# Normal rows and second-batch rows on VectorE instead of GpSimd, and two constant matmuls fewer, in an attention and mixture-of-experts kernel

## What is computed

```python
xn = _layernorm(x)
x = x + attention(xn) + ffn(xn)
# attention: 16 heads of 128, biases on q, k, v and o, causal softmax
# ffn(h):    x1 = rmsnorm(h, ln1_w); q, k with rotary embedding, 16 q heads, 4 k and v heads
#            r = h + causal_attention(x1) @ wo
#            y = rmsnorm(r, ln2_w); 4 of 32 experts for each token by softmax(y @ gate_w.T) + bias_e
#            r + sum of the weighted experts + one shared expert
```

## Time and profile before

| | |
|---|---|
| median of three runs | 797.4 us (795.85, 797.7, 797.4) |
| the profiled execution | 794.62 us, its span 792.8 us |
| mean granted TensorE clock | 0.986 |
| busy over the span | PE 750.2, DVE 539.9, ACT 489.9, POOL 494.1 us |
| chain that ended last, by engine | PE 76%, DVE 9%, ACT 6%, POOL 6% |
| normal rows on POOL (L621) | 8 rows, 1210 to 1228 ns each |
| second batch's rows on POOL (L607) | 4 rows, 1203 to 1814 ns each |
| first batch's rows on DVE (L1416) | 4 rows, 483 to 901 ns each |

### The profile page before, as it was taken

The page is one execution under the profiler, slowest core; times in us unless marked ns, Lnnn a source line. Parts: engine busy times, 40 slices in busy tenths (PEclk is TensorE's granted clock), DMA queues, the critical chain, the costliest instruction groups (busy, mean ns, idle before and its releaser), DMA issues.

```text
span 792.8 us, 14431 instructions
## 1 busy us (share of the span) xinstructions
PE 750.2 (95%) x4657; PEld 668.6 (84%) x4657; DVE 539.9 (68%) x1667; ACT 489.9 (62%) x1219; POOL 494.1 (62%) x564
## 2 busy tenths in 40 slices
PE   7759779999999999999998899999999999999997
PEld 4649669889888989888977788999999999999996
DVE  5647567979788797766678876665555565555564
ACT  3646557778777776667443566566556665566652
POOL 6957667867786778434433677366555865656553
PEclk9988999999999999999999999999999999999999
DMA  6000000000010129900100254077786777667634
GB/s 189 8 14 14 21 8 27 14 20 23 14 41 28 40 67 327 280 15 14 41 14 27 76 177 143 30 167 180 177 219 146 190 176 178 145 149 170 143 56 143
DMA packets 103523, 77.51 MB, mean 98 GB/s; under 512 B 6982, under 2 KB 102298, under 8 KB 103450
## 3 DMA queue, kind: packets, MB, share of 16 engines
q1 hardware_dynamic: 92114, 63.13, 27.7%
q0 software_dynamic: 10752, 12.74, 9.6%
q10 hardware_dynamic: 584, 0.73, 0.3%
HBM read 51.75 MB, written 24.82 MB: 97 GB/s over the span
## 4 chain that ended last, share of the span: by engine, by line
PE 76%; DVE 9%; ACT 6%; POOL 6%; issue 2%; DMA 1%; ACTq 0%; DVEq 0%; POOLq 0%
PE j L870 19%; PE ob L870 11%; PE zb L870 10%; PE s L870 10%; PE t L1011 7%; PE j L965 4%; ACT probs L1186 3%; PE j L973 2%; DVE probsT L1461 2%; PE zb L965 2%; PE ob L965 2%; POOL probs L700 1%; PE s L996 1%; POOL acc_a L621 1%; DVE probs L1446 1%
## 5 line engine op out<-in xcount | busy, mean ns | idle before, releaser
L700 POOL TENSOR_SCALAR probs<-probs,inv_sum 128x128 f32<-128x128 f32 x240 | 141.2, 600 | 152.8 <-DVE inv_sum L1452 148.1
L1186 ACT ACTIVATE probs<-probs,neg_max 128x128 f32<-128x128 f32 (+3 forms) x256 | 143.1, 559 | 126.9 <-DVE neg_max L1446 125.3
L1446 DVE CUSTOM_DVE_ANT_0 probs<-s,mask 128x128 f32<-128x128 f32 (+3 forms) x256 | 120.1, 485 | 40.4 <-PE s L996 27.4
L870 PE MATMUL s<-k_heads,q_heads 128*128 128x256 f32 (+2 forms) x576 | 140.6, 366 | 7.4 <-DVE neg_max L1446 7.0
L753 POOL DMA_INDIRECT moe_sum_dram<-late,slot_tokens x64 | 100.7, 1574 | 39.4 <-ACT late L1274 28.3
L1461 DVE TENSOR_TENSOR probsT<-t,probsT 128x384 fp32r<-128x384 f32 (+2 forms) x192 | 101.2, 548 | 11.1 <-ACT probsT L1201 11.0
L870 PEld LDWEIGHTS s<-k_heads,q_heads 128*128 128x128 f32 x576 | 93.2, 194 | 13.8 <-DVE neg_max L1446 10.0
L1201 ACT ACTIVATE probsT<-t 128x384 fp32r<-128x384 f32 (+2 forms) x192 | 90.1, 488 | 18.1 <-PE t L1011 17.8
L1011 PE MATMUL t<-ident,probs 128*128 128x128 f32 x640 | 94.7, 275 | 3.4 <-POOL probs L700 2.8
L1011 PEld LDWEIGHTS t<-ident,probs 128*128 128x128 f32 x640 | 74.8, 141 | 12.5 <-POOL probs L700 4.7
L870 PE MATMUL zb<-probsT,v_heads 128*128 128x512 f32 (+2 forms) x351 | 68.9, 340 | 1.4 <-DVE probsT L1461 0.9
(11 more groups left out here) (256 smaller groups left out, 1600.1 us busy)
## 6 DMA issues: line engine op xcount, KB each, us to landing
x_slots_dram<-mask SPq DMA_DIRECT2D x1, 8480.0 KB, 37.7
late<-x_slots_dram SPq DMA_DIRECT2D x32, 265.0 KB, 4.7
late<-in_L_ffn_weg_dram SPq DMA_DIRECT2D x64, 128.0 KB
late<-in_L_ffn_weu_dram SPq DMA_DIRECT2D x64, 128.0 KB
late<-in_L_ffn_wed_dram SPq DMA_DIRECT2D x64, 128.0 KB
moe_sum_dram<-mask SPq DMA_DIRECT2D x2, 1152.0 KB, 7.0
raw_qk<-in_L_ffn_wq_dram SPq DMA_DIRECT2D x16, 128.0 KB, 2.2
raw_o<-in_L_ffn_wo_dram SPq DMA_DIRECT2D x8, 256.0 KB, 2.7
```

The lines of the kernel that those rows point to most:

```text
L700: pool.tensor_scalar(piece, piece, rinv[:, u % 2, i:i + 1], 1.0, ALU.mult, ALU.mult).then_inc(p_norm, 1)
L870: m = pe.matmul(dst, lhs(a), rhs(b), start=first and i == 0, stop=last_ and i == 2, skip_group_check=skip)
L1186: act.activation(piece, piece, ACT.Exp, bias=nmax[:, u % 2, i:i + 1], scale=-1.0, accum_out=rsum[:, u % 2, i:i + 1]).then_inc(e_done, 1)
L1446: ve.tensor_tensor_reduce(pr[:, u % 2, P_OFF[i]:P_OFF[i] + width], bS[i % 2][:, 0:width], mask_t[:, S - width:S], INV_SCALE, BIG, ALU.add, ...
```

## The change

The rms rows of the second batch and the normal rows are written by VectorE. The two functions leave GpSimd's block and its `step`; on VectorE a function `rms_rows(b)` serves both batches and is called for batch 1 at the end of window -2, and `normal_rows(n)` stands in the rotary branch of `step`, ahead of `z_part(n)`. The semaphores `rows_of_b1` and `normal` are gone: the readers ask VectorE's own counter `ln_step`. The second call of `keep_busy`, with a count of two, is gone. The routing of tokens to experts is not touched.

```diff
@@ the numbers of VectorE's steps
-                    [(what, b) for what in ("var", "eps")] + [("xr", t) for t in tiles if b == 0]):
+                    [(what, b) for what in ("var", "eps")] + [("xr", t) for t in tiles]):
             LN[key] = len(LN) + 1
+    for t in range(NT):
+        LN["xn", t] = len(LN) + 1
@@ GpSimd
-            def second_rows(tiles):
-
-                for t in tiles:
-                    pool.tensor_scalar(xr[1][:, t - TB, :], accB[:, t, :], mv[:, t, 0:1], rstd[:, 1, t:t + 1],
-                                       ALU.subtract, ALU.mult).then_inc(rows_of_b1, 1)
-
...
-            def normal_rows(n):
-
-                if n in XN_UNITS:
-                    p = XN_UNITS.index(n)
-                    for t in (2 * p, 2 * p + 1):
-                        pool.tensor_scalar(accA[:, t, :], accB[:, t, :], mv[:, t, 0:1], rstd[:, 0, t:t + 1],
-                                           ALU.subtract, ALU.mult).then_inc(normal, 1)
...
                         first_powers(1)
                         q_sin(n, it)
-                        second_rows(range(TB, TB + 2))
                         q_lo(n, it)
-                        second_rows(range(TB + 2, NT))
                     weights(job, it)
...
                     normal_power()
-                normal_rows(n)
                 if n in (GS + 1, 2 * GS + 1):
                     pool.wait_ge(bc_in, 32)
-                    pool.wait_ge(normal, NT)
+                    pool.wait_ge(ln_step, LN["xn", NT - 1])
@@ TensorE
             last.then_inc(cx_mm, 1)
-            keep_busy(2)
...
-                        if b == 0:
-                            pe.wait_ge(ln_step, LN["xr", t])
-                        else:
-                            pe.wait_ge(rows_of_b1, t + 1)
+                        pe.wait_ge(ln_step, LN["xr", b * TB + t])
...
                 elif kind == "XN":
-                    pe.wait_ge(normal, 2 * v + 2)
+                    pe.wait_ge(ln_step, LN["xn", 2 * v + 1])
@@ VectorE
+            def rms_rows(b):
+
+                ve.wait_ge(ln_pow, b + 1)
+                for t in tiles_of(b):
+                    did(ve.tensor_scalar(xr[b][:, t - b * TB, :], accB[:, t, :], mv[:, t, 0:1], rstd[:, 1, t:t + 1],
+                                         ALU.subtract, ALU.mult), "xr", t)
+
+            def normal_rows(n):
+
+                if n in XN_UNITS:
+                    p = XN_UNITS.index(n)
+                    ve.wait_ge(ln_pow, B + 1)
+                    for t in (2 * p, 2 * p + 1):
+                        did(ve.tensor_scalar(accA[:, t, :], accB[:, t, :], mv[:, t, 0:1], rstd[:, 0, t:t + 1],
+                                             ALU.subtract, ALU.mult), "xn", t)
+
             variances(0)
-            ve.wait_ge(ln_pow, 1)
-            for t in range(TB):
-                did(ve.tensor_scalar(xr[0][:, t, :], accB[:, t, :], mv[:, t, 0:1], rstd[:, 1, t:t + 1],
-                                     ALU.subtract, ALU.mult), "xr", t)
+            rms_rows(0)
...
                         rope_sum(q, it)
                         k_lo(k, it)
+                        rms_rows(1)
                     if n == -1:
...
                 for ch in k_last:
                     k_lo(ch, it)
+                normal_rows(n)
                 z_part(n, it)
```

More of the change, by code:

```diff
@@ L375, in attention_pair_moe_kernel @@
         bias_added, table_in = sem("bias_added"), sem("table_loaded")
-        rows_of_b1, normal = sem("second_rows"), sem("normal_rows")
         cx_mm, cx_ev = sem("const_turned"), sem("const_kept")
```

## The result

| | before | after |
|---|---|---|
| median of four runs each, us | 796.62 (795.01 to 797.7) | 778.48 (778.03 to 778.96) |
| the profiled execution, us | 794.62 | 778.87 |
| its span, us | 792.8 | 777.1 |
| mean granted TensorE clock | 0.986 | 0.991 |
| busy PE / DVE / POOL, us | 750.2 / 539.9 / 494.1 | 747.7 / 548.3 / 478.8 |

The ratio after to before is 0.9774, interval [0.9753, 0.9795]: faster by 2.3%. The forecast was 777.4 us with a range of 773.5 to 785.0. By medians 18.1 us are gained where 20.0 were forecast; by the two profiled executions it is 15.75. What follows goes by those two executions, since only they have positions. One of the twelve executions of constants_only, in the experiments, took 941.65 us at a granted clock of 0.75 and is not in the ratio given there. L12 is now line 12 of the changed kernel, or of the kernel of the experiment.

The account below looks back on a forecast made before the run. TensorE was taken as bound by waits before 112 us, mostly for GpSimd's normal rows, and by its matmuls after. 12.8 + 5.5 + 1.3 + 0.4 = 20.0 us took the median from 797.4 to 777.4 us, range 773.5 to 785.0.

Parts of the forecast that it names:

- The normal rows: Units 0, 1, 4, 5: on VectorE at 0.65 us a row, TensorE's waits shrink to 0, 0.8, 0, 1.2; gain 12.8 us.
- The clock behind the waits: TensorE's clock stays high after the first, second and fourth turning of the normal rows; gain 5.5 us.
- I expect no fall after waits this short: At the turnings, waits of 0 to 1.2 us leave TensorE's clock high, so 3.45 us become 1.85 three times.
- The second batch's rows: At the start, moving four rows to VectorE brings the first mask forward and spares the last mask a wait; gain 1.3 us.
- 4 x 0.65 = 2.6 us: Four second-batch rows on VectorE before the first mask, which then starts at 23.5 instead of 24.29; gain 0.8 us.
- The second step: The second batch's last mask no longer waits for slow scores; gain 0.47 us.
- The two constants: At the start, without the two constant matmuls the first four transposes and projections come some 0.4 us sooner.
- The rival of the clock at the start: Without the constant matmuls TensorE's clock falls and the first two projections slow by 2.4 us; 780.6 us, chance 0.21.
- Blocking: Each new VectorE row must wait for the GpSimd instruction beside it, adding 1.2 us; 778.6 us, chance 0.18.
- The other rivals: TensorE's wait moves, 786.5 us, 0.12; VectorE becomes the bound, 808.2, 0.03; something else holds the transposes, 797.4, 0.04.
- The stages behind ... I let them shift whole: All gain falls within the first 112 us; later stages keep their own progress and lose none of the 20.0 us.
- three signs of being wrong: Clock of 0.5 between 9 and 16 us; waits over 2 us at the four places behind another engine; gain lost after 112.

Follow-up runs that it names:

- constants_only: The kernel before with only the two constant matmuls (second `keep_busy` call) taken out; 795.8 us, ratio 1.0013 to the kernel before.
- constants_back: The changed kernel with the two constant matmuls put back in their old place; 779.87 us, ratio 0.9804 to the kernel before.
- normal_only: The kernel before with only the normal rows moved from GpSimd to VectorE; 777.82 us, ratio 0.9771 to the kernel before.
- second_only: The kernel before with only the second batch's rows moved from GpSimd to VectorE; 795.02 us, ratio 0.9998 to the kernel before.
- change_again: The changed kernel run again unaltered, as yardstick on the same chip as two other kernels; 779.18 us, ratio 0.9802 to the kernel before.
- placed_no_constants: The changed kernel with second batch's rows behind the first two masks and normal rows behind the fourth, without constant matmuls; 773.98 us, ratio 0.9739 to the kernel before.
- second_late: Against constants_back: second batch's rows moved on VectorE behind the first two masks and the second q's sum; 802.17 us (slower chip), ratio 0.9769 to the kernel before.
- normal_early: The changed kernel with constant matmuls kept and normal rows moved on VectorE behind the fourth mask; 799.36 us (slower chip), ratio 0.9732 to the kernel before.
- placed_again: Same program as both_placed, on another chip: the changed kernel with both row moves on VectorE and constant matmuls kept; 774.52 us, ratio 0.9743 to the kernel before.
- before_weights: The kernel before with GpSimd writing the normal rows ahead of that unit's weights; 817.51 us (slower chip), ratio 0.9945 to the kernel before.
- both_placed: The changed kernel with both row moves on VectorE and constant matmuls kept, on the slower chip; 801.75 us, ratio 0.9748 to the kernel before.

## Why the prediction was right, and where it was not

**The normal rows: right.** Waits of 0, 0.8, 0 and 1.2 us against 0, 1.00, 0 and 1.49, so 12.3 us (14.8 - 2.5) where 12.8 stood. The row was priced too low: the pairs in front of the two waits took 1.41 and 1.51 us where 1.3 stood, which makes 0.3 of the 0.5 us.

**The clock behind the waits: right.** 12.8 + 5.5 = 18.3 us were forecast for both, and 17.9 came between 31.70 and 108.54, the same in the change, in constants_back and in normal_only. "I expect no fall after waits this short" held at the two turnings. It is no rule: behind 1.85 us before unit 0's later scores it fell in four executions of five.

**The second batch's rows: the steps fell.** "4 x 0.65 = 2.6 us" was 3.64, because each row waited for one of the four GpSimd instructions beside it, so the first mask gained nothing: 24.89 against 24.29. In constants_back, without the fall of the clock at the start, it is at 23.89, 0.4 us earlier, and 0.3 of that is an earlier start (its projections begin at 12.82 against 13.09). The second step, that the last mask "loses the 0.47 us that it waited for slow scores", took for granted that the scores would be fast. They were slow again, behind the new wait for the mask, and the last mask waited 0.71 us for them in the change and in constants_back. So where both clocks are low the term is 0.05 us (0.35 less the earlier start of 0.3), not 1.3. second_only has 1.2 (1.46 - 0.3), but 1.1 of it is the clock that stayed high there: that the term looks nearly right in that execution is luck. The prediction named VectorE as late next there, and did not ask what this wait does to TensorE's clock.

**The two constants: the sign was wrong in the trace, and nothing can be measured in the time.** The rival of the clock at the start came true. The profile shows 0.50 from 12 to 14 us, the sign that I had named. It costs 1.0 us in the ledger, where the rival's terms were 2.4 + 0.4 for the fall and 0.4 for the gain that goes with it. The first projection takes 2.63 us, but the second 1.55 already, not 2.84 twice, and the slower constant matmul ahead of them was hidden: they begin at 12.79, and at 12.82 in constants_back. So the 0.4 us that leaving out the constants was to bring did not come either, since the last row held back the transposes in both: they end at 11.43 and 11.46. In four of four profiled executions without these constants the clock fell at the start (the change, constants_only, change_again, placed_no_constants); in seven of nine with them it stayed up, and in the other two it had fallen in a late DMA's wait before them. In placed_no_constants it is at 0.50 from 9 us on, behind a DMA's wait of 1.51 us and before its third transpose, so the transposes can hardly be all of the cause there; with a wait of 1.45 us and the constants the kernel before kept it up. The Trainium skill (TensorE: Matmul & The Clock Gate, "Part 4: PE-mode transpose") holds that transposes don't count as busy time for the gate in the way that matmuls do. The traces are in line with it: the change had eight transposes between 8.71 and 11.43 and a clock of 0.50 behind them. They don't prove it, since it also idled for 0.49 and 0.40 us among them.

**Blocking: the rival was right as a mechanism.** It was priced at 1.2 us on top of rows of 0.65. "Against it: 0.65 holds such waits already" was true of the earlier trace rows: those four rows end at 8.61, 9.01, 9.84 and 10.57, each 0.15 us after a GpSimd instruction (8.46, 8.87, 9.69, 10.42). But these took 0.4 to 0.8 us, and beside the new rows stand some of 1.0 to 1.3. The moves away from GpSimd's work gave more. Against constants_back, second_late has 1.75 us more at 31.70 (2.10 - 0.35) and normal_early 2.8 us more from there to 108.54 (20.65 - 17.89): some 4.5 us in all, and 4.7 to 5.2 by the times. It is not all blocking: 1.1 us are the clock that no longer falls, and the masks and the turnings also gain by the new order of the list. The estimate above gives blocking up to 1.5 of the 2.5 us at the turnings; no run parts the two. The Trainium skill (SBUF — State Buffer, "Who interferes with whom") has it as an exclusive lock between GpSimd and a VectorE operation that uses two ports. The traces agree: 0.40 us a row where GpSimd is idle, up to 1.35 where it works.

**The other rivals** fell. At the turnings no wait took the place of those removed, beyond the 2.5 us; VectorE did not become the bound; and nothing else held the transposes.

**"The stages behind ... I let them shift whole": not quite.** Of the three signs of being wrong two came: the clock of 0.5 between 9 and 16 us, and a loss behind 112 us. A part of the gain was lost again after 112 us: of 17.23 us at 108.54, 15.34 are left at 392.39. The section below shows the place. The medians differ by 18.1 us and the profiled executions by 15.75. I had added 2.8 us to the sum to come from the profiled execution before to the median; after the change the profiled execution is no longer below the median (778.87 against 778.48). So in the profile's own terms 20.0 us of gain were forecast and 15.75 came. The 4.25 between them are, by the ledger: 1.4 at the constants (-1.0 for 0.4), 0.95 at the second batch's rows (0.35 for 1.3), 0.4 at the normal rows, and 1.5 lost later. That the median fell within 1.1 us of the forecast (778.48 against 777.4) is in good part luck: two of the four terms did not come, 1.5 us were lost later, and the 2.8 us for the distance between profile and median, which was not there after the change, covered most of it.

## What to carry to other kernels

Price a VectorE row of this kind by what GpSimd does beside it, not by one mean: here it ended 0.15 us after the GpSimd instruction beside it. Look for the stretch where GpSimd waits, and put the row there. When a wait of a microsecond or two moves from one place to another, ask at the new place too what TensorE's clock does behind it. And compare two traces at a landmark that comes once in each stage: it shows in one table which edit paid, and what is lost again far behind it.

## What the runs showed that I had not expected

**The clock fell with no idle time at all.** In the change 32 small matmuls (32 columns each) multiply the gate's columns, one behind the other:

```profile
366.48 3.69 PE L910 MATMUL j<-gate_cols,late 128*128 128x32 f32 x32
369.98 2.91 PE L850 MATMUL j<-xnT,w_qk 128*128 128x512 f32 x6
```

and the clock behind them (columns as above):

```profile
370.00:374.00 4.00, 4.00 (x13) 3.20 (x13) 1.30 (x4) 0.58 (x1) 2.60 (x6) 0.58 0.10 30
```

The same place in constants_back:

```profile
366.03 3.65 PE L911 MATMUL j<-gate_cols,late 128*128 128x32 f32 x32
369.52 1.63 PE L851 MATMUL j<-xnT,w_qk 128*128 128x512 f32 x6
```

TensorE has no idle row in either, and six projections take 2.91 us in the one and 1.63 in the other. Of the thirteen profiled executions six fell here (the change, change_again, normal_only, placed_again, before_weights, both_placed), at 1.6 us each, and 3.2 in both_placed. It comes back alike in the two executions of the changed kernel, and none of the three edits goes with it. What decides it is open.

**A blocked row on VectorE ends 0.14 to 0.15 us after the GpSimd instruction beside it** (24.97 and 24.82, 40.05 and 39.91, 23.76 and 23.62), and this holds without exception. Over the thirteen profiled executions VectorE wrote 160 such rows. 54 took 0.40 to 0.41 us, and each of the other 106 ended 143 to 153 ns after a GpSimd instruction. A row that started first was not held up: in the pair at 49.55 the first took 407 ns, though `q_lo` began at 49.68 beside it, and the second, blocked, 1089.

**One chip stood still in the middle.** The 25 us of the slower chip lie at one place. At the scores that the kernel before (on its own chip) starts at 431.22, second_late is 20.13 us ahead of it; at 473.14 it is 8.48 us behind, and stays so. ScalarE there, in order of time:

```profile
449.34 0.69 ACT L1215 ACTIVATE k_heads<-j,const_cols 128x512 fp32r<-128x512 f32 x1 [7.18 <-remote]
457.81 0.69 ACT L1192 ACTIVATE zT<-ob,const_cols 128x512 fp32r<-128x512 f32 x1 [7.17 <-remote]
```

The engines wait for something that the profile doesn't attribute to any of them ("remote"), in the profiles of all four kernels on that chip and in none of the others. Its cause is open: nothing was tried for it.
